# The masking instruction of an attention row leaves the row's negative maximum itself

## The reference, cut to what matters

```
def attn_map(qi, ki):
    s = jnp.einsum('bqhd,bkhd->bhqk', qi, ki) * scale
    s = jnp.where(causal, s, neg)
    return jax.nn.softmax(s, axis=-1)
p1 = attn_map(q[:, :, :, 0], k[:, :, :, 0])
p2 = attn_map(q[:, :, :, 1], k[:, :, :, 1])
lam = lam1 - lam2 + LAMBDA_INIT
p = p1 - lam * p2
```

## Time and profile before

| | us |
|---|---|
| median of 3 runs (1369.73 to 1370.14) | 1369.96 |
| the profiled execution's own time | 1370.52 |
| its span, first to last instruction | 1368.7 |
| TensorE busy | 1351.8 |
| VectorE busy | 1026.2 |
| ScalarE busy | 888.6 |
| GpSimd busy | 868.3 |

### The profile page before, as it was taken

How to read it: one execution, slowest core, us unless ns; L and a number is a source line. 1 busy time by engine, 2 the same in 40 slices (tenths; PEclk the granted TensorE clock), 3 DMA queues, 4 the chain that set the end, 5 groups by cost and what they waited for, 6 DMA issues and landing times.

```text
span 1368.7 us, 26497 instructions
## 1 busy us (share of the span) xinstructions
PE 1351.8 (99%) x8342; PEld 1206.2 (88%) x8342; DVE 1026.2 (75%) x2589; ACT 888.6 (65%) x2494; POOL 868.3 (63%) x1352
## 2 busy tenths in 40 slices
PE   9999999999999999999999999999999999999998
PEld 8898999889988999889889999889899888888787
DVE  8877777777787777876877777866777888856545
ACT  5666667765676766765676666665667777765441
POOL 2766666655666666655676656646767878777443
PEclk9999999999999999999999999999999999999999
DMA  4000000000000000000000000000100000000001
GB/s 144 24 1 1 1 2 1 16 1 1 32 1 2 1 1 1 17 1 1 32 1 1 1 1 1 20 1 1 47 1 1 24 25 1 17 32 1 28 17 35
DMA packets 9752, 18.50 MB, mean 14 GB/s; under 512 B 912, under 2 KB 7312, under 8 KB 9104
## 3 DMA queue, kind: packets, MB, share of 16 engines
q1 hardware_dynamic: 8272, 15.23, 3.3%
q10 hardware_dynamic: 1344, 1.57, 0.3%
HBM read 14.71 MB, written 2.10 MB: 12 GB/s over the span
## 4 chain that ended last, share of the span: by engine, by line
PE 86%; DVE 6%; POOL 4%; ACT 2%; issue 2%; DMA 1%; SPq 0%; ACTq 0%; POOLq 0%; DVEq 0%
PE turn_bank L720 9%; PE score_bank L698 8%; PE score_bank L700 8%; PE score_bank L699 8%; PE score_bank L815 7%; PE turn_bank L722 5%; PE sum_bank L720 5%; PE turn_bank L707 4%; PE proj_bank L720 3%; PE proj_bank L766 3%; PE turn_bank L780 3%; PE sum_bank L722 2%; PE turn_bank L766 2%; PE sum_bank L707 2%; PE proj_bank L780 2%; PE proj_bank L707 2%
## 5 line engine op out<-in xcount | busy, mean ns | idle before, releaser
L850 ACT ACTIVATE e<-score_bank,negmx 128x512 f32<-128x512 f32 (+2 forms) x640 | 395.0, 627 | 85.8 <-DVE negmx L1068 84.5
L1313 POOL TENSOR_TENSOR e<-e,e 128x512 f32<-128x512 f32 (+3 forms) x256 | 294.7, 1151 | 21.4
L1064 DVE TENSOR_REDUCE mx<-score_bank 128x1 f32<-128x512 f32 (+1 forms) x384 | 242.1, 638 | 41.4 <-PE score_bank L700 40.0
L698 PE MATMUL score_bank<-k_hi,q_hi 128*128 128x512 f32 (+2 forms) x640 | 258.7, 404 | 2.7 <-ACT e L850 2.2
L1296 POOL TENSOR_TENSOR inv_s<-s,neg_one 128x1 f32<-128x1 f32 x128 | 70.6, 551 | 280.8 <-DVE s L1280 280.7
L720 PE MATMUL turn_bank<-v_hl,pT_hi 128*128 128x512 f32 x633 | 230.2, 398 | 1.8 <-DVE pT_lo L1074 1.3
L700 PE MATMUL score_bank<-k_hi,q_lo 128*128 128x512 f32 (+2 forms) x640 | 231.5, 362 | 0.0
L699 PE MATMUL score_bank<-k_lo,q_hi 128*128 128x512 f32 (+2 forms) x640 | 231.2, 361 | 0.0
L1310 POOL TENSOR_SCALAR e<-e,ratio 128x512 f32<-128x512 f32 (+3 forms) x256 | 181.2, 708 | 12.0
L1059 DVE CUSTOM_DVE_ANT_0 score_bank<-score_bank,mask 128x384 f32<-128x384 f32 (+3 forms) x256 | 143.4, 560 | 50.2 <-PE score_bank L700 48.7
L722 PE MATMUL turn_bank<-v_hl,pT_lo 128*128 128x256 f32 x633 | 177.4, 280 | 0.0
(11 more groups left out here) (377 smaller groups left out, 3492.3 us busy)
## 6 DMA issues: line engine op xcount, KB each, us to landing
w_raw<-in_w_qkv_dram SPq DMA_DIRECT2D x3, 1024.0 KB, 4.9
w_raw<-in_w_o_dram SPq DMA_DIRECT2D x4, 512.0 KB, 3.3
w_raw<-in_w_ug_dram SPq DMA_DIRECT2D x4, 512.0 KB, 4.2
bv<-in_hidden_dram SPq DMA_DIRECT2D x8, 256.0 KB, 3.0
out_dram<-e SPq DMA_DIRECT2D x16, 128.0 KB, 1.7
e<-in_w_d_dram SPq DMA_DIRECT2D x1, 1024.0 KB, 4.9
x_in<-in_hidden_dram SPq DMA_DIRECT2D x2, 256.0 KB, 3.8
x_in<-in_hidden_dram ACTq DMA_DIRECT2D x2, 256.0 KB, 4.3
```

Of the source, the lines that this page charges most:

```text
L698: pe.matmul(bank[:, 0:w], qh, kh, start=True, stop=False)
L850: act.activation(e, S[k % NS][:, 0:w], ACT.Exp, bias=negmx[:, d % 2, m, s:s + 1], accum_out=ssum[:, d % 4, s, m, c:c + 1]).then_inc(s_act, 1)
L1064: dve.tensor_reduce(mx[:, d % 2, m, s, c:c + 1], S[k % NS][:, 0:w], X, ALU.max)\
L1313: pool.tensor_tensor(a, a, b, ALU.add).then_inc(p_pool, 1)
```

## The change

The masking instruction reduces with min in place of max, over scores that it negates with its factor of -1, and leaves the result in `negmx` at once. The reduction's start value takes in the other chunks of the row: a constant for a row of one chunk; the first chunk's value in `mx`, read through a pointer, for a row of two; and for rows of three and four chunks the minimum over `mx`, which a small reduce makes ahead of the masking instruction and which that instruction waits for. The chunk maxima of the earlier chunks are stored negated. The last chunk's scores stand negated in their bank, so its exponential takes a scale of -1. ScalarE waits for the masking instruction's semaphore `s_dve`. Two empty lines and renames of the semaphore in its lists are left out of the diff.

```diff
-LOWEST = -3e38
+HIGHEST = 3e38
...
                 def exponentials(exps):
                     for d, m, j in exps:
-                        o, s, _, c, w, _ = duo_chunks(d)[j]
+                        o, s, _, c, w, last = duo_chunks(d)[j]
                         q, k = CHUNKS * d + j, s_use(d, m, j)
-                        act.wait_ge(neg_ready, 4 * d + 2 * m + o % 2 + 1)
+                        act.wait_ge(s_dve, s_use(d, m, max(jj for jj, ch in enumerate(duo_chunks(d)) if ch[0] == o)) + 1)
...
                         act.activation(e, S[k % NS][:, 0:w], ACT.Exp, bias=negmx[:, d % 2, m, s:s + 1],
-                                       accum_out=ssum[:, d % 4, s, m, c:c + 1]).then_inc(s_act, 1)
+                                       scale=-1.0 if last else 1.0, accum_out=ssum[:, d % 4, s, m, c:c + 1]).then_inc(s_act, 1)
...
+                n_least = 0
                 for kind, what, _, factors, mixes in with_lags(steps, VECTOR_LAGS):
                     if kind == "S":
                         d, m, j = what
                         _, s, _, c, w, last = duo_chunks(d)[j]
                         k = s_use(d, m, j)
+                        least = HIGHEST
+                        if last and c == 1:
+                            dve.wait_ge(s_dve, k)
+                            least = mx[:, d % 2, m, s, 0:1]
+                        elif last and c > 1:
+                            dve.wait_ge(s_dve, k)
+                            least = mx[:, d % 2, m, s, 3:4]
+                            dve.tensor_reduce(least, mx[:, d % 2, m, s, 0:c], X, ALU.min).then_inc(least_ready, 1)
+                            n_least += 1
                         dve.wait_ge(s_full, k + 1)
                         if last:
                             if d == 0:
                                 dve.wait_ge(mask_ready, 1)
+                            if c > 1:
+                                dve.wait_ge(least_ready, n_least)
                             dve.tensor_tensor_reduce(out=S[k % NS][:, 0:w], in0=S[k % NS][:, 0:w],
-                                                     in1=mask[:, BANK - w:], scale=1.0, scalar=LOWEST,
-                                                     op0=ALU.add, op1=ALU.max,
-                                                     accum_out=mx[:, d % 2, m, s, c:c + 1]).then_inc(s_dve, 1)
+                                                     in1=mask[:, BANK - w:], scale=-1.0, scalar=least,
+                                                     op0=ALU.add, op1=ALU.min,
+                                                     accum_out=negmx[:, d % 2, m, s:s + 1]).then_inc(s_dve, 1)
                         else:
-                            dve.tensor_reduce(mx[:, d % 2, m, s, c:c + 1], S[k % NS][:, 0:w], X, ALU.max)\
-                               .then_inc(s_dve, 1)
-                        if last:
-                            dve.wait_ge(s_dve, k + 1)
-                            dve.tensor_reduce(negmx[:, d % 2, m, s:s + 1], mx[:, d % 2, m, s, 0:c + 1], X,
-                                              ALU.max, negate=True).then_inc(neg_ready, 1)
+                            dve.tensor_reduce(mx[:, d % 2, m, s, c:c + 1], S[k % NS][:, 0:w], X, ALU.max,
+                                              negate=True).then_inc(s_dve, 1)
```

More of the change, by code:

```diff
@@ L488, in build @@
              s_full, s_act, s_dve, t_full, t_hi, t_lo, r_full, r_hi, r_free, kv_full, kv_act, kv_dve, v_lo,
-             neg_ready, sums_ready, ratio_step, ratio_ready, e2_scaled, p_pool, p_dve, pv_done, o_half_ready, o_ready,
+             least_ready, sums_ready, ratio_step, ratio_ready, e2_scaled, p_pool, p_dve, pv_done, o_half_ready, o_ready,
              msq_ready, rms_step, rms_ready) = semaphores(
@@ L493, in build @@
                 "lam_ready", "b_ready", "w_hi", "w_lo", "s_full", "s_act", "s_dve", "t_full", "t_hi", "t_lo", "r_full",
-                "r_hi", "r_free", "kv_full", "kv_act", "kv_dve", "v_lo", "neg_ready", "sums_ready", "ratio_step",
+                "r_hi", "r_free", "kv_full", "kv_act", "kv_dve", "v_lo", "least_ready", "sums_ready", "ratio_step",
                 "ratio_ready", "e2_scaled", "p_pool", "p_dve", "pv_done", "o_half_ready", "o_ready", "msq_ready",
```

## The result

| | before | after |
|---|---|---|
| median, us | 1370.06 | 1373.42 |
| range | 1369.73 to 1370.30 | 1372.96 to 1373.87 |
| the profiled execution's own time | 1370.52 | 1372.96 |

The changed kernel is slower: 3.36 us, ratio 1.0025 with a 95% interval of 1.0017 to 1.0032. The two profiled executions differ by 2.44 us only, since the one of after is the fastest of its runs and the one of before lies 0.5 over its median. One run further down, of the kernel with short rows only in the new form, took 2219.4 us at a granted TensorE clock of 0.557; the range given there leaves it out.

A forecast was written before the change was run, and what follows sets the result against it. TensorE, busy 1351.8 of 1368.7 us, was taken to bound the kernel. Long-row losses of +1.75 and +0.56 less gains of 1.03 gave +1.3 on the median 1369.96: 1371.3 us, range 1367.8 to 1374.3 for 8 in 10.

The forecast's parts named there:

- What an instruction and a wait cost: On VectorE: unblocked work overlaps by 0.08 us; a predecessor wait costs 0.12, or 0.21 if not named first.
- Rival 1: On VectorE, a wait on the predecessor costs nothing and no new stall forms: about -1.5, 1368.5 us; chance 0.12.
- Pointer, small reduce, signs: Added on VectorE: pointer 0.06 us in 192 rows; front reduce 0.29 or 0.41 unless hidden, in 128; signs 0.
- Rival 4: The masking instruction's pointer costs far more than 0.06; at 0.3, some 20 late places, +6, 1376 us; chance 0.06.
- Removed: The small reduce behind the mask goes, 256 times: exponential 0.19 us sooner, VectorE frees the same 0.19.
- What reaches TensorE: At score products, lateness against bank cover: +1.75 and +0.56 lost, -1.03 gained, sum +1.3 us.
- the eleven late places: Long rows with less cover than lateness before score products: seven lose 0.25 us each, four 0.14.
- rival 2: Late long rows delay ScalarE's later copies and the next row; 24 places at 0.25 give +5, 1375 us; chance 0.15.
- The gains: Rows of one and two chunks shorten TensorE stalls by 0.19 or 0.13 us each, together -1.0.
- rival 3: A quarter of 12 us of earlier short-row exponentials reaches TensorE, long-row reduces mostly hidden: -3.5, 1366.5 us; chance 0.12.
- What would show it: Signs in the changed profile: gaps, instruction times, ScalarE waits, TensorE stalls; wrong if TensorE's idle time moves over 3 us.

The follow-up runs named there:

- all-old: Against the changed kernel, all 256 rows have the small reduce behind the mask again, signs and scales kept: 1370.17 us, ratio 1.0000.
- long-rows-new: Against the changed kernel, rows of one and two chunks have the small reduce behind the mask again: 1376.08 us, ratio 1.0045.

## Why the prediction was right or wrong

**The costs on VectorE and the two directions were right, and the time is inside the range, but over the forecast by 2.1 us.** It is past the 2.7 us that I had set as the bound of "no change" (0.63), so it fell to "slower", which I had given 0.23. What reaches TensorE was mis-sized on both sides, and the errors had opposite signs: that the time came inside the range is in part luck.

**What an instruction and a wait cost: right.** Independent work starts 0.083 before the record in front ends, dependent work 0.035 behind it, and the mask 0.145 behind the small reduce in 91 of the 128 rows (I had 0.13); in 34 of the other 37 it waits for its scores and starts later still. Against an unblocked start this is 0.12 for a wait on the instruction in front and 0.23 where that wait isn't named first, and 3.5 us hang on which wait stands first (1369.89 against 1373.42). Rival 1 falls with it.

**Pointer, small reduce, signs: right.** 624 against 566 ns is the 0.06 (756 against 697 in 512 columns, 484 against 425 in 256). Signs: 0. Rival 4 falls. What the pointer alone costs the long rows of their 6.0 us, no run shows.

**Removed: right for the exponential, small for VectorE.** The exponential starts 0.04 behind the read, and the row of two chunks gains 0.13 as said. VectorE frees 0.24, not 0.19: the product of the earlier trace rows started 0.24 behind the read's start and now starts with it (386.01 twice).

**"What reaches TensorE", the eleven late places: the step that failed on the loss side.** The listed places were right: the same product's start in all-old and in long-rows-new kernels moves by 0.14 to 0.39 at each, 2.8 in sum against the 2.3 counted. But I compared each row's lateness with the cover of its own score bank only, and wrote of the transposes' low parts that they "have enough cover". Ten more places lose 2.5 together (near 262, 297, 372, 560, 595, 670, 858, 893, 1111 and 1127), and none is among my eleven. The one at 373 is shown above: an unbroken ScalarE hands the 0.28 to `wo_hi`, a waiting VectorE takes it over, and it surfaces 6 us later as a late low part. Near 297 I read the same beginning (ScalarE 0.35 later, with no gap, from 293.6 to 296.2). The traces settle the last step of all ten. None is a score product: in the changed kernel, in the one with all long rows new and in the one with those of the first map TensorE starts 0.15 behind the end of a VectorE record, a `pT_lo` at six (262, 372, 560, 670, 858, 1111), an `o_sum` at three (297, 595, 893), an `oT_lo` at the last. At 262, 560 and 858 an exponential of ScalarE ends 0.84 before the product in all three, at 297, 595 and 893 one ends 0.97 before it, so there too the lateness comes over ScalarE; at 1111 and 1127 its way is open. At those eight it is rival 2's mechanism, and all ten with the eleven make 21 places where rival 2 had 24; its 1375 failed because the gains were larger as well.

**The gains: the step that failed on the other side.** -1.0 counted, -3.1 measured. In the second map a sooner maximum also makes the ratio sooner on GpSimd, and the mix in front of a later mask, so the row at 417.9 gave 0.32 in place of 0.13. I had counted stalls by their own row alone. In the last group (960 to 1150 us) short rows gave 1.3 us, of which I had only the 0.13 at 1082; which rows the rest came from is open. The 5.8 us of waits that I held against rival 3 count four stalls twice, once for the weight load and once for the product, and TensorE gained more than it had waited for exponentials. Rival 3 asked for a quarter of 12 us, 3.0: that quarter did arrive, but its other half, hidden reduces in long rows, did not.

**What no step had: the exchanged order at 1172 us**, +1.05 at that place, 1.2 by experiment. It is set off by a change of 0.40 in the offset between two engines. The same exchange costs the kernel with short rows only 0.7 near 65 us, where a mix of 384 columns on VectorE takes 1.68 in place of 0.62; the changed kernel has none there.

So the sum was short by errors of both signs: losses by 3.6, gains by 2.8 (2.1, and the 0.7 that the exchange near 65 us hides), the exchange at 1172 us by 1.2. They make 2.0 together; measured it is 2.1. By its interval each measured part is known only to 1 or 2 us, so that they close this well proves little.

**What would show it.** Of the signs that I named, the 0.13 behind the small reduce, 624 and 566 ns, and the longer stalls held (at 387 +0.26, 278 +0.27). Of 417.9 the size was off. "ScalarE's wait down 5 us in short rows and up in long ones" came out as +5 over both. TensorE's idle time grew by 2.5 us (19.4 in place of 16.9), within the 3 us that I had named.

**The version that beats both.** Rows of one and two chunks in the new form and long rows in the old one: 1366.93 us, 3.1 below the kernel before.

## What to carry to other kernels

A shortening and a lengthening of the same chain don't cancel: find out by kind of row which side each is on, and keep the change only where it shortens. Follow lateness through each engine that has no idle time behind it, to the next engine that waits there, until it reaches one with a gap or the one that bounds the kernel; the nearest consumer alone accounted here for about half of it. And where a fresh result is waited for with older ones, name it first; here that was worth 3.5 us.

## What the runs showed of the hardware that was not expected

- The wait that the mask of a long row names second has a record of its own in front of it. In the trace of after it is the wait for the small reduce (L1072, `EVENT_SEMAPHORE`, 128 times, 21 ns at the median; in the row shown at 385.23, ahead of the mask at 385.33). With the two lines exchanged it is the wait for the scores (L1069, 21 ns; at 275.34, ahead of the mask at 275.52), in 126 of the 128 rows. Named first, the fresh wait lets the mask start 0.03 behind the small reduce's end, named second 0.14.
- The accumulator read of 0.14 us starts at the same time as the next independent instruction, in 198 of 256 rows: its record overlaps by its full length (386.01 twice above).
- When VectorE and GpSimd both work on two SBUF tiles of 512 float32 columns, the second to start pays, in each of the two cases shown: VectorE 0.68 becomes 1.65, GpSimd 1.29 becomes 1.61. A change of 0.4 us in the offset of the two moved a microsecond to TensorE.
